# Cross-attention on one core: x and context loaded by columns, scales from column maxima, two buffers of split operands, and the attention loop's first loads moved into the last projection batch

## The chip, the cores and the metric

The kernel runs on one core of a Trainium2 chip. The metric is the device time in microseconds of one execution, the median of several.

## What is computed

The reference (shapes B = 8 batches, S = 512 rows of x, C = 320, T = 508 text tokens and 4 image tokens of E = 512, H = 20 heads of D = 16), cut to what matters:

```
text_ehs, ip_ehs = ctx[:, :-4], ctx[:, -4:]
q, k_t, v_t = heads(x @ W_q), heads(text_ehs @ W_k), heads(text_ehs @ W_v)
probs_t = softmax(q k_t^T * D**-0.5)
text_out = probs_t v_t
k_ip, v_ip = heads(ip_ehs @ W_k_ip), heads(ip_ehs @ W_v_ip)
qsem = l2norm(probs_t @ text_ehs);  sem = qsem @ l2norm(ip_ehs)^T
probs_ip = softmax(q k_ip^T * D**-0.5 + 0.5 * sem) * spatial_mask
out = (text_out + probs_ip v_ip) @ W_out + b_out + x
```

## The kernel before

The work has three phases, one after the other on every engine. Every engine has its program written out by hand and the engines meet at counting semaphores.

*Phase 1*, a loop over the 8 batches. x and the context of a batch are loaded by rows (SP, `x_sb`, `ctx_sb`), transposed on TensorE (fp32 against an identity, `XT_JOB`, `CT_JOB`), and each transposed tile is split on its way out of PSUM into two fp16 parts: ACT writes the high part times a scale (L700, L703), VectorE the remainder (L1017, L1020), into `x_t` and `ctx_t`, of which there is one each. The scale of a batch bounds its largest row norm: VectorE sums squares by row (`squares`, L908) in the v stage of the batch before, TensorE turns the row maxima into a row (`tops`, L1220), VectorE and ACT make scales of it on one partition, and TensorE spreads these over the partitions with a matmul against ones (`scales`, L1232). TensorE's products (L1286) are three fp16 matmuls for each pair of tiles (high by high, high by low, low by high): q (27 matmuls of 512 columns), k (36 of 508), v with the token columns (48 of 324), then the fp32 image token scores (L1344), then the Gram products of the context with itself (48 of 508 to 127 columns) and the transposes of the Gram blocks (L1374). q and k leave as three bf16 parts: ACT the first (L733, L736), VectorE the residual (L1032, `residual`), ACT the middle (L723, `middle`), GpSimd the last (L546); SP stores them, v and the Gram matrix u to DRAM. ACT copies the transposed Gram blocks into `u_sb` (L779).

PSUM's eight banks are given out by hand: a job (j, n) is the n-th use of bank j in a batch, `use` turns it into a count, and TensorE waits in `free` until the bank's use before is drained. The Gram transposes (`GT_JOB`) use bank 3, the first q tile bank 0.

*Phase 2*, the attention, 640 units of 128 rows of one head: scores (L1394), exp on ACT, transposes, then products with v and u. Between the phases SP waits for the stores of parts, v and u, then loads the first two groups of heads, their values and two Gram matrices, with an issue for each copy (`load_group`, L362 and L366); ACT waits for the same three stores. *Phase 3* is the image token softmax and the output projection.

Of the kernel before, what the change touches and what calls it, by code (L numbers as in the profile page):

```python
# [5 lines left out]
def xattn_kernel(  # L6
    nc: bass.Bass,
    x: bass.AP,
    ctx: bass.AP,
# [34 lines left out]
    E = ctx.shape[2]  # L44
    N_IP = 4
    T = ctx.shape[1] - N_IP
# [12 lines left out]
    NC = len(CT)  # L59
    HIP = H * N_IP  # L60
# [28 lines left out]
    with stack:  # L89
# [9 lines left out]
        ones_row = sb("ones_row", [1, P], fp32)  # L99
# [12 lines left out]
        scale = sb("scale", [P, 4], fp32)  # L112
# [3 lines left out]
        x_sb = sb("x_sb", [P, 2, ST, C], fp32)  # L116
# [6 lines left out]
        discard = sb("discard", [P, 2, E], fp32)  # L123
# [12 lines left out]
        q_ring = work[0:KS, 0:2 * GROUP * S // 2].bitcast(bf16).rearrange("p (n h s) -> p n h s", n=2, h=GROUP)  # L136
        k_ring = x_sb[0:KS, :, :, :].rearrange("p r s c -> p (r s c)")[:, 0:2 * GROUP * T // 2].bitcast(bf16)\
# [5 lines left out]
        sumsq = sb("sumsq", [P, TT + ST], fp32)  # L143
        row_max = sb("row_max", [P, 2], fp32)
        w_sums = sb("w_sums", [P, 3], fp32)
        w_scale = sb("w_scale", [P, 3], fp32)
        top = sb("top", [1, 2, 2], fp32)
        w_top = sb("w_top", [1, 3, 3], fp32)
        scale_row = sb("scale_row", [1, 5], fp32)
        w_row = sb("w_row", [1, 3], fp32)  # L150
# [10 lines left out]

        ctx_sb = carve(P, TT * E).rearrange("p (k e) -> p k e", k=TT)
        ctx_t = carve(P, ET * T).bitcast(fp16).rearrange("p (a e t) -> p a e t", a=2, e=ET)
        x_t = carve(P, NC * S).bitcast(fp16).rearrange("p (a c s) -> p a c s", a=2, c=NC)
# [37 lines left out]

        consts_made = sem("consts_made")
# [4 lines left out]
        wq_padded = sem("wq_padded")  # L208
# [3 lines left out]
        w_sums_ready = sem("w_sums_ready")  # L212
        w_top_ready = sem("w_top_ready")
        w_root_ready = sem("w_root_ready")
        w_row_ready = sem("w_row_ready")
        w_hi_split = sem("w_hi_split")
        w_split = sem("w_split")
        top_ready = sem("top_ready")
        top_root_ready = sem("top_root_ready")
        in_hi_split = sem("in_hi_split")  # L220
        ipn_hi_split = sem("ipn_hi_split")
# [13 lines left out]
        sumsq_ready = sem("sumsq_ready")  # L235
        row_max_ready = sem("row_max_ready")
        scale_row_ready = sem("scale_row_ready")
# [49 lines left out]
        FIRST_USES = [0, 0, 0, 0, 0, 0, 0, 4]  # L287
        IP_USES, IP_AFTER = [1, 1, 1, 1, 0, 0, 0, 0], 2
        USES = [3, 3, 3, 3, 3, 3, 3, 4]
# [5 lines left out]
        W_TOP, TOP_0, W_SCALE, SCALE_0 = (7, -3), (7, -2), (7, -1), (7, 0)  # L295
        K_JOB = [(3, 2), (4, 2), (5, 2)]
        V_JOB = [(6, 2), (2, 3), (0, 3), (1, 3)]
        IPS_JOB = (7, 1)
        G_JOB, GT_JOB = [(4, 3), (5, 3), (6, 3), (7, 4)], (3, 3)
# [17 lines left out]
        CTX_COL, X_COL, Q_COL, K_COL = range(4)  # L317
        V_DOWN, SEM_DOWN = 2.0 ** -16, 2.0 ** -13
# [6 lines left out]
        IN_TILES = NC + ET  # L325

        CONSTS = 13 + 1 + D
# [45 lines left out]
        def _(sp):  # L373
            x_in = x.rearrange("b (s p) c -> b p s c", p=P)

            def load_ctx(b):
                for k in range(TT):
                    sp.dma_start(ctx_sb[:, k, :], ctx[b, k * TP:k * TP + P, :]).then_inc(ctx_loaded, 16)

            sp.dma_start(x_sb[:, 0], x_in[0]).then_inc(x_loaded, 16)  # L380
            load_ctx(0)
            for b in range(B):
                sp.dma_start(ip_rows[b * N_IP:(b + 1) * N_IP, 0, :], ctx[b, T:T + N_IP, :]).then_inc(ip_loaded, 16)
# [3 lines left out]
            def store_batch(b):  # L387
# [8 lines left out]

                sp.wait_ge(sem_step, 2 * (b + 1))
# [7 lines left out]
            def next_batch(b):  # L405

                sp.wait_ge(bank_filled[XT_JOB[-1][0]], use(XT_JOB[-1], b))
                sp.dma_start(x_sb[:, 0], x_in[b + 1]).then_inc(x_loaded, 16)
                sp.wait_ge(bank_filled[CT_JOB[-1][0]], use(CT_JOB[-1], b))
                load_ctx(b + 1)  # L410
                store_batch(b)

            sp.wait_ge(row_max_ready, 1)
            next_batch(0)
            with sp.Fori(1, B - 1) as b:
                next_batch(b)


            store_batch(B - 1)
            sp.wait_ge(parts_saved, 1 + 16 * 2 * NC * B)  # L420
            sp.wait_ge(v_saved, 1 + 16 * B)
            sp.wait_ge(u_saved, 1 + 16 * B)
            sp.wait_ge(bank_filled[IPS_JOB[0]], use(IPS_JOB, B - 1))
            for n in range(2):
                load_group(sp, 0, n, n)
                load_values(sp, 0, n, n)
            for par in range(2):
                sp.dma_start(u_sb[:, par, :], u_parts[par]).then_inc(u_loaded, 16)
# [66 lines left out]
        def _(pool):  # L495
# [24 lines left out]
            for d in range(D):  # L520
                if d:
                    pool.wait_ge(consts_made, 14 + d)
# [126 lines left out]
        def _(act):  # L649
# [41 lines left out]
            def batch(b, first, last):  # L691
# [13 lines left out]
                if first:  # L705
                    weight_first(wk, wk_raw, 0)
                    weight_first(wvx, wv_raw, 1)
# [826 lines left out]
```

## Time and profile before

| | us |
|---|---|
| median of 3 runs (lowest, highest) | 1804.03 (1801.88, 1806.68) |
| the profiled execution | 1804.91 |
| its span, first to last instruction | 1803.2 |
| first scores of phase 2 start at | 349.1 |
| TensorE matmul busy, whole span | 1736.2 |
| VectorE, ACT, GpSimd busy, whole span | 1244.6, 1182.8, 1230.7 |

PE is TensorE's matmuls, PEld its weight loads (they overlap), DVE is VectorE, POOL is GpSimd, SP the engine that issues most transfers, an engine's name with a q its sequencer. Busy is the sum of instructions' times. L12 is line 12 of the kernel. PEclk is the granted clock of TensorE as a share of full speed, 1.0 for 2.4 GHz and 0.5 for 1.2 GHz.

### The profile page before, as it was taken

Reading aid. Unit: us, or ns where it says so; the run is one execution under the profiler, and the core shown is the slowest. Engines: PE = TensorE matmul, PEld = TensorE weight load, DVE = VectorE, ACT = ScalarE, POOL = GpSimd, SP = SyncE. Lnnn points to the kernel's source line nnn. Section 1 sums busy time; section 2 is a strip of 40 time slices with the busy share of each in tenths; the row PEclk is TensorE's granted clock in tenths of the full one; section 3 lists DMA queues with packets and bytes.
Section 4 is the critical chain, followed back from the end, with each engine's and each line's share of the span. In section 5 each row is a group of like instructions: output and inputs, shape, how many; then the busy total and the mean of one; then the engine's idle time right before and its main releaser. Section 6 shows DMA issues by size and latency. Waiting matters only on the chain.

```text
span 1803.2 us, 48758 instructions
## 1 busy us (share of the span) xinstructions
PE 1736.2 (96%) x14421; PEld 1103.9 (61%) x14421; DVE 1244.6 (69%) x2872; ACT 1182.8 (66%) x2644; POOL 1230.7 (68%) x1414
## 2 busy tenths in 40 slices
PE   4999999599999999999999999999999999999899
PEld 2767666466666666665666666656566666666455
DVE  5445554277777777777777777767677777777684
ACT  2455455477777777777777777777777777777321
POOL 2122212388888888888788888878888888888310
PEclk7999999799999999999999999999999999999999
DMA  5445554734566445445555555465555445553133
GB/s 161 113 139 142 137 144 123 171 68 92 101 103 119 92 91 111 92 91 92 105 92 100 99 121 92 91 106 92 90 90 113 93 91 103 104 96 66 37 103 101
DMA packets 429986, 187.83 MB, mean 104 GB/s; under 512 B 387128, under 2 KB 417472, under 8 KB 429792
## 3 DMA queue, kind: packets, MB, share of 16 engines
q1 hardware_dynamic: 427488, 183.41, 49.4%
q10 hardware_dynamic: 2304, 2.14, 0.4%
q8 instruction: 84, 1.38, 0.3%
q14 instruction: 110, 0.90, 0.2%
HBM read 67.21 MB, written 34.39 MB: 56 GB/s over the span
## 4 chain that ended last, share of the span: by engine, by line
POOL 37%; PE 35%; issue 22%; DVE 3%; POOLq 1%; ACT 1%; DMA 0%; SPq 0%; ACTq 0%; DVEq 0%
POOL probs L586 16%; POOL probs L593 16%; PE bank L1286 13%; PE bank L1429 6%; PE bank L1430 4%; PE bank L1494 3%; POOL reduced L601 2%; POOL wkv L579 2%; PE bank L1344 2%; PE bank L1394 2%; PE bank L1403 1%; PE bank L1495 1%; POOL reduced L600 1%; PE bank L1434 1%; DVE reduced L1017 1%
## 5 line engine op out<-in xcount | busy, mean ns | idle before, releaser
L1429 PE MATMUL bank<-u_sb,late 127*128 127x508 f16 x2560 | 944.0, 375 | 0.0
L1430 PE MATMUL bank<-u_sb,late 127*128 127x508 f16 (+3 forms) x2560 | 761.1, 297 | 0.0
L1090 DVE TENSOR_REDUCE neg_max<-bank 128x1 f32<-128x508 f32 x640 | 439.3, 687 | 342.0 <-PE bank L1394 341.7
L579 POOL TENSOR_TENSOR wkv<-probs,wkv 128x508 f16<-128x508 f32 x320 | 358.8, 1121 | 199.6 <-ACT wkv L816 199.6
L1428 PE MATMUL bank<-v_ring,late 127*128 127x41 f16 x2560 | 468.1, 183 | 4.4 <-DVE late L1105 4.4
L1099 DVE SCALAR_TENSOR_TENSOR probs<-bank,probs 128x508 f32<-128x508 f32 x640 | 432.9, 677 | 4.6 <-PE bank L1430 4.6
L1428 PEld LDWEIGHTS bank<-v_ring,late 127*128 127x128 f16 x2560 | 246.7, 96 | 233.4 <-DVE late L1105 4.5
L593 POOL TENSOR_TENSOR probs<-probs,late 128x508 f32<-128x508 f32 x320 | 368.6, 1152 | 0.0
L586 POOL TENSOR_TENSOR probs<-probs,wkv 128x508 f32<-128x508 f32 x320 | 357.6, 1118 | 0.0
L1429 PEld LDWEIGHTS bank<-u_sb,late 127*128 127x128 f16 x2560 | 247.8, 97 | 166.2 <-issue 1.1
L1394 PE MATMUL bank<-x_sb,work 96*128 96x508 bf16 x640 | 241.8, 378 | 28.2 <-DMA x_sb<-k_parts 12.2
L1430 PEld LDWEIGHTS bank<-u_sb,late 127*128 127x128 f16 x2560 | 244.8, 96 | 0.0
L807 ACT ACTIVATE probs<-bank,neg_max 128x508 f32<-128x508 f32 x320 | 216.8, 677 | 38.7 <-DVE neg_max L1090 20.8
L796 ACT ACTIVATE exp_bias<-neg_max 128x1 f32<-128x1 f32 x320 | 64.7, 202 | 257.1 <-DVE neg_max L1090 257.1
L1105 DVE SCALAR_TENSOR_TENSOR late<-bank,late 127x512 f16<-127x512 f32 x320 | 219.5, 686 | 7.5 <-ACT late L832 7.5
L816 ACT ACTIVATE wkv<-probs 128x508 f16<-128x508 f32 x320 | 201.4, 629 | 25.1 <-ACT probs L807 17.4
L807 ACT ACTIVATE probs<-bank,exp_bias 128x508 f32<-128x508 f32 x320 | 216.2, 676 | 0.0
L1403 PEld LDWEIGHTS bank<-ident,probs 128*127 128x127 f32 x1280 | 190.9, 189 | 9.2
L823 ACT ACTIVATE late<-probs 128x508 f16<-128x508 f32 x320 | 195.8, 612 | 0.7
L1403 PE MATMUL bank<-ident,probs 128*127 128x128 f32 x1280 | 195.1, 275 | 0.0
L546 POOL TENSOR_TENSOR late<-work,late 128x512 bf16<-128x512 f32 (+3 forms) x48 | 55.2, 1151 | 202.9 <-ACT late L723 202.9
L832 ACT ACTIVATE late<-bank 127x512 f16<-127x512 f32 x320 | 184.9, 578 | 0.0
(166 smaller groups left out, 1803.7 us busy)
## 6 DMA issues: line engine op xcount, KB each, us to landing
x_sb<-k_parts SPq DMA_DIRECT2D x192, 79.4 KB, 3.5
x_sb<-in_x SPq DMA_DIRECT2D x16, 640.0 KB, 5.0
reduced<-in_ctx SPq DMA_DIRECT2D x32, 256.0 KB, 5.1
work<-q_parts SPq DMA_DIRECT2D x32, 240.0 KB, 3.4
u_parts<-u_sb SPq DMA_DIRECT2D x8, 825.5 KB, 4.2
u_sb<-u_parts SPq DMA_DIRECT2D x8, 825.5 KB, 5.4
v_parts<-v_sb SPq DMA_DIRECT2D x8, 820.0 KB, 8.0
v_ring<-v_parts SPq DMA_DIRECT2D x32, 205.0 KB, 3.7
```

What stands on the lines that cost most here:

```text
L579: nc.gpsimd.tensor_tensor(rows[:, 1, :, 0:TP], probs[:, j % PROB_RING, :].rearrange("p (k t) -> p k t", k=TT), rows[:, 0, :, 0:TP], ALU.su ...
L586: nc.gpsimd.tensor_tensor(own, own, flat_rows(at(rnd, j)[1])[:, 1, :, 0:TP], ALU.add).then_inc(odd_weight_ready, 1)
L593: nc.gpsimd.tensor_tensor(own, own, half_hi[:, at(rnd, j)[1] // 2 % RING, :], ALU.subtract).then_inc(even_weight_ready, 1)
L807: nc.scalar.activation(probs[:, j % PROB_RING, :], bank[S_BANK + j % 2][:, 0:T], ACT.Exp, bias=bias[:, j % 4:j % 4 + 1]).then_inc(probs_re ...
L1090: nc.vector.tensor_reduce(neg_max[:, j % 4:j % 4 + 1], bank[S_BANK + j % 2][:, 0:T], AX.X, ALU.max, negate=True)\
L1099: nc.vector.scalar_tensor_tensor(own, bank[Y_BANK + j % 2][:, 0:T], 1.0 if j % 2 == 1 else 2.0 * PROB_SCALE, own, ALU.mult, ALU.mult, accu ...
L1286: last = nc.tensor.matmul(out, stationary(a), moving(m), start=(n == 1), stop=(n == len(SPLIT) * len(terms)))
L1394: nc.tensor.matmul(bank[S_BANK + j % 2][:, 0:T], q_ring[:, n, h, st * P:(st + 1) * P], k_ring[:, n, h, :], start=True, stop=True).then_inc ...
L1403: last = nc.tensor.transpose(bank[PT_BANK + j // 2 % 2][0:TP, k * P:(k + 1) * P], probs[:, j % PROB_RING, k * TP:(k + 1) * TP], ident[:, :])
L1428: nc.tensor.matmul(o, hi_k, v_ring[0:TP, n, h, k, :], start=(k == 0), stop=False)
L1429: nc.tensor.matmul(y, hi_k, u_sb[0:TP, par, GH[k]:GH[k] + T], start=(k == 0), stop=False)
L1430: done = nc.tensor.matmul(y[:, k * TP:T], hi_k, u_sb[0:TP, par, UL[k]:UL[k] + U_COLS[k]], start=False, stop=(k == TT - 1))
```

## The change

- x comes twice: by rows as before for the last addition, and by columns (`x_cols`, three tiles of 128 columns, of which the third holds the last 64 columns twice). The context comes by columns without the image tokens (`ctx_cols`), the image tokens as an input of their own, W_q in three row tiles like x. The layout is made before the launch. The input transposes, their banks and waits go; raw tiles lie in `raw`.
- A batch's scale comes from the absolute maxima of its columns: VectorE reduces both raw tiles after the third residual of the batch before (`column_sums`), squares and adds them by partition, and one matmul against a 128 x 128 of ones (`spread_sums`) adds over partitions, behind the k products. VectorE bounds the sums (`find_top`), ACT takes the root, VectorE makes scales on all partitions.
- `x_t` and `ctx_t` exist twice. The next batch is split in the v stage, two ACT instructions and three of VectorE. The third x tile holds high parts on 64 partitions and remainders on the other 64, so a q tile takes 8 matmuls for 9. The batch loop's body is written out for two batches.
- The jobs are renumbered: Gram transposes go to bank 0, which the next batch's first q tile uses as well.
- SP loads batch b + 2 between the stores of batch b's parts and of its v, and in the last batch the first heads, values and the first Gram matrix of phase 2; the second Gram matrix is loaded in phase 2's first round. ACT enters phase 2 after the stores of the parts alone.
- In the start, the weights' scales go the same way, and VectorE begins without GpSimd's masks.

```diff
-        Q_JOB = [(0, 2), (1, 2), (2, 2)]
-        XT_JOB = [(0, 1), (1, 1), (2, 1)]
-        CT_JOB = [(3, 1), (4, 1), (5, 1), (6, 1)]
-        TOP_JOB, SCALE_JOB = (7, 2), (7, 3)
-        G_JOB, GT_JOB = [(4, 3), (5, 3), (6, 3), (7, 4)], (3, 3)
+        SCALE_JOB = (7, 1)
+        Q_JOB = [(0, 1), (1, 1), (2, 1)]
+        K_JOB = [(3, 1), (4, 1), (5, 1)]
+        V_JOB = [(6, 1), (0, 2), (1, 2), (2, 2)]
+        IPS_JOB = (7, 2)
+        G_JOB, GT_JOB = [(3, 2), (4, 2), (5, 2), (6, 2)], (0, 3)
...
+            def load_columns(b):
+                sp.dma_start(raw_x, x_cols[b]).then_inc(x_loaded, 16)
+                sp.dma_start(raw_ctx, ctx_cols[b]).then_inc(ctx_loaded, 16)
...
+            def columns_of(b):
+                sp.wait_ge(in_lo_split, 2 * b)
...
+                load_columns(b)
+            def first_heads():
+                sp.wait_ge(in_lo_split, 2 * B)
+                sp.wait_ge(parts_saved, 1 + 16 * 2 * NC * (B - 1))
+                sp.wait_ge(v_saved, 1 + 16 * (B - 1))
+                sp.wait_ge(u_saved, 1 + 16 * (B - 1))
+                load_group(sp, 0, 0, 0)
+                load_values(sp, 0, 0, 0)
+                sp.dma_start(u_sb[:, 0, :], u_parts[0]).then_inc(u_loaded, 16)
+                load_group(sp, 0, 1, 1)
+                load_values(sp, 0, 1, 1)
+            columns_of(1)
+            store_batch(0, lambda: columns_of(2))
+            with sp.Fori(1, B - 2) as b:
+                store_batch(b, lambda: columns_of(b + 2))
+            store_batch(B - 2, lambda: None)
+            store_batch(B - 1, first_heads)
...
+            def split_x(b, par):
+                act.wait_ge(scale_ready, b + 1)
+                nc.scalar.activation(x_t[par][:, 0], raw_x, ACT.Identity, scale=scale[:, par, X_COL:X_COL + 1]).then_inc(in_hi_split, 1)
...
             act.wait_ge(parts_saved, 1 + 16 * 2 * NC * B)
-            act.wait_ge(v_saved, 1 + 16 * B)
-            act.wait_ge(u_saved, 1 + 16 * B)
...
+            def column_sums(b):
+                dve.wait_ge(x_loaded, 16 * (b + 1))
+                nc.vector.tensor_reduce(col_max[:, ET:IN_TILES], raw_x, AX.X, ALU.max, apply_absolute_value=True).then_inc(stat_step, 1)
+                dve.wait_ge(ctx_loaded, 16 * (b + 1))
+                nc.vector.tensor_reduce(col_max[:, 0:ET], raw_ctx, AX.X, ALU.max, apply_absolute_value=True).then_inc(stat_step, 1)
+                dve.wait_ge(stat_step, 2 * (b + 1))
+                for col, (c0, c1) in ((CTX_COL, (0, ET)), (X_COL, (ET, IN_TILES))):
+                    nc.vector.scalar_tensor_tensor(col_squares[:, c0:c1], col_max[:, c0:c1], 1.0, col_max[:, c0:c1], ALU.mult,
+                                                   ALU.mult, accum_out=sums[:, col:col + 1]).then_inc(sums_ready, 1)
...
                 for t in range(NC):
                     residual(t)
+                if not last:
+                    column_sums(b + 1)
                 for t in range(NC, 2 * NC):
                     residual(t)
+                if not last:
+                    find_top(SCALE_JOB, b, 0, 2)
...
                     if k == 1 and not last:
-                        squares(b + 1)
+                        make_scales(b + 1, 1 - par)
+                    if k == 2 and not last:
+                        split_x(b + 1, 1 - par)
+                if not last:
+                    split_ctx(b + 1, 1 - par)
...
+                pe.wait_ge(in_lo_split, 2 * b + 1)
                 for m, (c0, cn) in enumerate(CT):
                     j = Q_JOB[m]
-                    pe.wait_ge(bank_drained[XT_JOB[-1][0]], use(XT_JOB[-1], b))
                     free(j)
...
+                free(SCALE_JOB)
...
+                    pe.wait_ge(sums_ready, 2 * (b + 2))
+                    spread_sums(SCALE_JOB, 0, 2)
```

## Rows read from the trace of the kernel before

**Rows 1.** Busy time of each engine and granted clock, by stretch of the span

```profile
core 0: us, PE busy (x) PEld busy (x) DVE busy (x) ACT busy (x) POOL busy (x), PEclk, DMA share, GB/s
31.90:43.90 12.00, 11.96 (x28) 3.27 (x29) 8.06 (x14) 6.27 (x9) 1.15 (x1) 0.51 0.00 0
...
59.20:336.30 277.10, 273.72 (x1668) 190.51 (x1667) 136.11 (x393) 138.61 (x317) 66.26 (x86) 0.98 0.49 133
```

**Rows 2.** The chain that ended last, 150 to 160 us: start, us, what

```profile
151.37 0.31 PE bank L1232 x2
...
154.66 0.50 ACT u_sb L779
...
157.09 0.74 DVE reduced L1017
```

**Rows 3.** Timeline of TensorE: start, us, engine, line, out<-in, [idle before <-releaser]

```profile
121.53 6.54 PE L1286 MATMUL bank<-reduced,wq 128*128 128x512 f16 x27 [0.31 <-DVE reduced L1017]
...
146.42 2.79 PE L1286 MATMUL bank<-reduced 128*127 128x508 f16 x12
...
154.29 1.50 PE L1295 MATMUL bank<-ident,x_sb 128*128 128x128 f32 x12
...
157.88 6.54 PE L1286 MATMUL bank<-reduced,wq 128*128 128x512 f16 x27 [0.34 <-DVE reduced L1017]
164.35 8.01 PE L1286 MATMUL bank<-reduced,wkv 128*128 128x508 f16 x36
172.29 6.83 PE L1286 MATMUL bank<-wkv,reduced 128*127 128x324 f16 x48
```

**Rows 4.** Timeline of all engines, the last batch's Gram stage

```profile
329.78 6.74 PE L1286 MATMUL bank<-reduced 128*127 128x508 f16 x48
...
336.96 0.93 ACT L779 ACTIVATE u_sb<-bank 127x127 f16<-127x127 f16 x3
```

**Rows 5.** Groups of instructions: busy us, mean ns of one

```profile
L1090 DVE TENSOR_REDUCE neg_max<-bank 128x1 f32<-128x508 f32 x640 | 439.3, 687 | 342.0 <-PE bank L1394 341.7
...
L968 DVE SCALAR_TENSOR_TENSOR wkv<-probs,w_scale,wkv 128x1280 f16<-128x1280 f32 x1 | 1.5, 1535 | 0.0
...
L677 ACT ACTIVATE wkv<-probs,w_scale 128x1280 f16<-128x1280 f32 x1 | 1.4, 1371 | 0.0
...
L968 DVE SCALAR_TENSOR_TENSOR wq<-probs,w_scale,wq 128x960 f16<-128x960 f32 x1 | 1.2, 1219 | 0.3 <-ACT wq L677 0.3
L677 ACT ACTIVATE wq<-probs,w_scale 128x960 f16<-128x960 f32 x1 | 1.1, 1094 | 0.7 <-DVE w_scale L962 0.7
```

**Rows 6.** Timeline of all engines, the third residual of a batch

```profile
165.75 0.74 DVE L1032 SCALAR_TENSOR_TENSOR work<-bank,scale,late 64x512 f32<-64x512 f32 x1 [1.41 <-ACT late L733]
```

**Rows 7.** Who waited for whom, whole span: us in total, times, longest us

```profile
ACT v_sb L749 <- PE bank L1286: 37.1, 32, 8.7
...
DVE top L916 <- PE bank L1220: 28.4, 8, 5.2
ACT ip_scores L757 <- PE bank L1344: 26.9, 8, 3.6
...
PE bank L1394 <- issue: 8.6, 3, 3.3
```

**Rows 8.** Timeline of all engines, the start of the kernel

```profile
2.57 0.78 ACTq L653 DMA_DIRECT2D reduced<-in_L_xattn_W_v  x1
...
51.83 0.43 PE L1253 MATMUL bank<-ident,reduced 32*128 32x32 f32 x4
...
59.18 9.19 PE L1286 MATMUL bank<-wkv,reduced 128*127 128x324 f16 x48
```

**Rows 9.** DMA issues: KB each, median us to landing

```profile
reduced<-in_L_xattn_W_v ACTq DMA_DIRECT2D x1, 640.0 KB, 12.3
```

**Rows 10.** The chain that ended last, 300 to 360 us

```profile
337.91 3.54 DMA u_parts<-u_sb
...
349.10 0.60 PE bank L1394
```

**Rows 11.** Timeline of TensorE, the Gram stage of the sixth batch

```profile
255.65 4.22 PE L1286 MATMUL bank<-reduced 128*127 128x508 f16 x12
```

More of the change, by code:

```diff
@@ L98, in xattn_kernel @@
         ident16 = sb("ident16", [P, P], fp16)
[L99 removed]
+        ones = sb("ones", [P, P], fp32)
         headmask = sb("headmask", [P, NC, H], fp32)
@@ L111, in xattn_kernel @@
         vw = sb("vw", [96, B, C], fp32)
-        scale = sb("scale", [P, 4], fp32)
+        scale = sb("scale", [P, 2, 4], fp32)
         kept_scale = sb("kept_scale", [P, B, 2], fp32)
@@ L403, in store_batch @@
                 sp.dma_start(u_parts[b], u_sb[:, 1, :]).then_inc(u_saved, 16)
[L405 to L428, printed above, removed]
+            def columns_of(b):
+                sp.wait_ge(in_lo_split, 2 * b)
+                apart(sp)
+                load_columns(b)
[15 more added lines that the diff above has]
+            store_batch(B - 1, first_heads)
             sp.wait_ge(flat_padded, 1)
@@ L670, in _ @@
+            act.wait_ge(w_scale_ready, 1)
+            weight_first(wq, wq_raw, WQ_COL)
+            split_x(0, 0)
+            act.wait_ge(bank_drained[W_JOB[0]], use(W_JOB, 0))
+            nc.scalar.activation(bound[:, 3:5], top[:, 3:5], ACT.Sqrt, scale=IN_TOP ** -2).then_inc(w_root_ready, 1)
+            split_ctx(0, 0)
+            act.wait_ge(w_scale_ready, 5)
+            weight_first(wk, wk_raw, WK_COL)
             act.wait_ge(ip_step, 1)
             nc.scalar.activation(ip_stat[:, 1:2], ip_stat[:, 0:1], ACT.Sqrt).then_inc(ip_root, 1)
-            act.wait_ge(wq_padded, 1)
@@ L688, in ip_tokens, with batch @@
                 act.wait_ge(bank_drained[1], ip_use(1))
-            def batch(b, first, last):
-                act.wait_ge(bank_drained[SCALE_JOB[0]], use(SCALE_0, 0) if first else use(SCALE_JOB, b - 1))
-                apart(act)
-                for t in range(IN_TILES):
-                    j = (XT_JOB + CT_JOB)[t]
-                    act.wait_ge(bank_filled[j[0]], use(j, b))
-                    if t < NC:
-                        cn = CT[t][1]
-                        nc.scalar.activation(x_t[0:cn, 0, t, :], bank[j[0]][0:cn, 0:S], ACT.Identity,
-                                             scale=scale[0:cn, X_COL:X_COL + 1]).then_inc(in_hi_split, 1)
-                    else:
-                        nc.scalar.activation(ctx_t[:, 0, t - NC, :], bank[j[0]][:, 0:T], ACT.Identity,
-                                             scale=scale[:, CTX_COL:CTX_COL + 1]).then_inc(in_hi_split, 1)
-                if first:
-                    weight_first(wk, wk_raw, 0)
-                    weight_first(wvx, wv_raw, 1)
+            def batch(b, par, first, last):
                 def ip_columns():
@@ L772, in batch @@
                                              scale=2.0 * GRAM_SCALE).then_inc(gram_hi2_split, 1)
-                    if k == 0 and not last:
-                        scale_root(b + 1)
                 act.wait_ge(bank_filled[GT_JOB[0]], use(GT_JOB, b))
@@ L1306, in batch, with products @@
-                if first:
-                    first_scales()
+                def products(out, terms, more=()):
+                    pairs = [(stationary(a), moving(m)) for stationary, moving in terms for a, m in SPLIT] + list(more)
+                    for n, (stationary, moving) in enumerate(pairs):
+                        last = nc.tensor.matmul(out, stationary, moving, start=(n == 0), stop=(n == len(pairs) - 1))
+                    return last
+                x_b, ctx_b = x_t[par], ctx_t[par]
@@ L1376, in batch @@
                 last.then_inc(bank_filled[GT_JOB[0]], 1)
-            batch(0, True, False)
-            with pe.Fori(1, B - 1) as b:
-                batch(b, False, False)
-            batch(B - 1, False, True)
+            batch(0, 0, True, False)
+            with pe.Fori(0, B // 2 - 1) as pair:
+                for par in (1, 0):
+                    batch(2 * pair + 2 - par, par, False, False)
+            batch(B - 1, 1, False, True)
             for j in range(8):
```

407 lines of the change are left out of this document (178 added, 229 removed).

## The prediction

> **What bounds the kernel now.** I read the busy share by stretch first, then the chain that ended last where one batch of the first phase gives way to the next. From 59.2 to 336.3 us TensorE is busy 273.72 of 277.1 us at a granted clock of 0.98 [rows 1]: the batch loop is TensorE's. The second phase and the projections are not edited, so the question is what leaves TensorE's own stream in the first 349 us, and what it waits for then.
>
> The chain at a boundary [rows 2] runs ACT's copies of the transposed Gram blocks (L779, to 154.66 + 0.50 = 155.16), ACT's first split, VectorE's remainders (L1017, to 157.09 + 0.74 = 157.83), TensorE. TensorE's timeline of the batch [rows 3] fills that in: the input transposes start at 154.29, the q products at 157.88, the k products at 164.35, the v products at 172.29. One undisturbed batch takes 157.88 - 121.53 = 36.35 us.
>
> **The change, part by part.**
>
> *The batch boundary.* Transposes, their PSUM banks and the splits that follow them leave the boundary; the split operands wait in the other buffer. But the q products of the next batch now use bank 0 right after the Gram transposes, which have moved from bank 3 to bank 0. So TensorE no longer waits for VectorE, but for ACT's L779 copies. Where that ends when no scale work sits between the Gram products is shown by the last batch, which has none already: Gram products start at 329.78, L779 ends at 336.96 + 0.93 = 337.89 [rows 4], 8.11 us; with 0.06 us of release the next q products can start 8.17 us after the Gram start. Before it was 157.88 - 146.42 = 11.46 us [rows 3]. Gain 3.29 us for each of 7 boundaries, 23.0 us. About 1 us of idle TensorE stays in each.
>
> *q products.* 9 matmuls per output tile become 8 (the third row tile carries x's high part and its remainder on 128 partitions). 27 of them take 164.35 - 157.88 = 6.47 us [rows 3], 0.240 us each; the share of pure streaming is less, so I take 0.22 us for each of the 3 removed: 0.65 us in each of 7 batches, 4.6 us.
>
> *Scales.* Two matmuls with the ones move behind the k products, where nothing else hides them: 0.31 us as the chain gives for the old pair, L1232 [rows 2]. It was inside the 11.46 us and is gone from the 8.17, so it counts again: 6 x 0.31 = 1.9 us lost (batch 0's belongs to the start).
>
> *VectorE in the k stage.* The column maxima need reductions of 3 x 512 and 4 x 508 elements. The nearest row is the 128x508 reduction at 687 ns [rows 5]; its elements at the rate by which two VectorE rows differ ((1535 - 1219) / 320 = 0.98 ns an element) leave some 0.19 us fixed, so 1.7 + 2.2 us, with two short operations 4.4 us. They stand between the third and the fourth residual. The third ends 165.75 + 0.74 = 166.49 [rows 6], 2.1 us after the k products begin; so the sums are ready 6.5 us after it, and TensorE, which wants them after 7.94 us, has 1.4 us of slack. Queued behind them are residuals 4 to 6, ACT's middle parts of these and GpSimd's L546; residual 6 waits for the last k product anyway. Bounds for the reductions: 2.0 us (twice as fast as the row) costs nothing less, as they are off TensorE's path; at twice the price (7.9 us) TensorE stands 2.6 us a batch.
>
> *The splits in the v stage.* ACT gets 1536 and 2032 elements; by L677 (1094 ns for 960, 1371 for 1280 [rows 5]) 1.6 + 2.0 us. VectorE gets 1.3 + 0.7 + 2.3 us by L968, and loses the seven remainders of L1017 and L1020 and the squares of L908. Cover: ACT now waits 37.1 us in 32 waits for v products and 26.9 in 8 for the token scores, 8.0 us a batch; VectorE 28.4 in 8 for the old maxima [rows 7]. In us after the k start: the four v tiles are filled 1.7 apart (6.83 / 4 [rows 3]) from 9.9 on; the scales stand behind VectorE's work on the second, about 13.7; ACT's x split to 15.3, two v tiles 16.5, context split 18.5; VectorE's x remainders to 18.4, the fourth tile 19.1, context remainders 21.3. The token scores are full when the Gram products start, 146.42 - 121.53 - 6.47 + 0.3 = 18.7 [rows 3], and VectorE is wanted one Gram tile and two copies later, about 22.5. So ACT has 0.2 us of slack there and more behind, since its next tile is 2.6 us off, VectorE 1.2. If that cover goes, each us over reaches TensorE through L779.
>
> *Loads.* Two issues in place of five, some 1.78 MB, behind the parts' stores and ahead of the v store on SP's queue. They leave at about 21.3 us after the k start and are read some 14 us later; a wait there would hold SP's v and u stores too, and ACT awaits those only a batch later. I price it at nothing.
>
> *Start of the kernel.* VectorE no longer waits for GpSimd's masks. The last thing late is w_v: issued at 2.57 us, 12.3 us to landing [rows 8, 9], 14.9; with 0.2 MB more ahead, 15.3. Squares 1.5 us (16.8), four short scale operations (17.2), ACT's w_q split 1.1 and x split 1.6 (19.9), VectorE's x remainders 2.0: q products at 22.0 instead of 31.9. Their 27 filled a stretch of 12.0 us at clock 0.51 [rows 1]; 24 take 10.7 us, to 32.7. If the clock again rises some 11.7 us into the stretch, the k products, 7.94 us (172.29 - 164.35), lose 0.5 us: 41.1. Scale matmuls 41.4; token work 51.83 to 59.18 [rows 8], 7.35 us: 48.8. Gain 59.18 - 48.8 = 10.4 us.
>
> *Into the second phase.* L779 ends at 337.89; then come the u store's 3.54 us, its issues and loads, and the first scores at 349.10 [rows 10]. Now SP issues the first two groups, values and u in the last v stage (some 10 us of issues from 324 on), done before the Gram products end; ACT waits for the parts' stores alone. The first scores follow the last drains: 338.0. Gain 11.1 us. The v store starts some 5 us later, and nobody waits for it but SP's later load. What is late next is the pipeline fill up to the first unit, 12.3 us on ACT and GpSimd, which stays.
>
> **Sum.** 10.4 + 23.0 + 4.6 - 1.9 + 11.1 = 47.2 us. Profiled execution: 1804.91 - 47.2 = 1757.7. It lies 0.9 us over the median of 1804.03; from there 1756.8. I take 1757.
>
> **The clock.** The trace has cold spells beside the start: at 255.65 twelve Gram products took 4.22 us against 2.79 [rows 11, 3], 1.4 us lost; batch 1 had one too, and batch 0 lost 9.19 - 6.83 = 2.4 us in its v stage [rows 8, 3]. The sum keeps three such spells. The Trainium skill (TensorE: Matmul & The Clock Gate, HAM oscillation — how this bites in real kernels) describes a kernel whose clock falls again at every tile because TensorE waits for data in each one; a wait in each batch is what this change leaves. Its section Part 4: PE-mode transpose says that transposes don't count as busy for the clock as other matmuls do, which speaks the other way, since transposes are what goes. By the first the sum would be 40, by the second alone 47 or a little more; no row here separates them.
>
> **Rivals.**
> 1. *The clock falls in every batch* (0.17). For: the new 1 us idle follows the Gram transposes, close on low-activity work. Against: TensorE idles 0.34 us there already [rows 3], and the spells begin elsewhere, at the token scores. Five more, 5 x 1.43 = 7.2 us: 1764.
> 2. *VectorE becomes the bound of the k stage* (0.10): reductions slower than the row, at double price 7 x 2.6 = 18 us back: 1775. Against: two VectorE forms agree on the rate.
> 3. *The doubled loop body costs instruction supply, or the first phase's early loads collide* (0.08). TensorE stood 8.6 us in 3 waits for nothing but issue in the second phase [rows 7]; three such in the new pair loop give 8.6 us: 1766. Against: the old batch loop shows none.
> 4. *Slower than before* (0.03): the same place as rival 2, the column sums late, whether by the reductions or because the loads land late. The price per batch must exceed the slack by 47.2 / 7 = 6.7 us, that is column sums ending 8.1 us later than reckoned, 12.5 us for 4.4. At 14 us: 7 x (14 - 4.4 - 1.4) = 57 back, 1814. The loads of before (x and context together) landed within some 8 us of their first issue, far inside 14.
>
> My forecast has 0.62. **Range.** Likeliest case alone: 1753 to 1761 (start within 2 us either way, spells from one to five). With rivals 1 and 3 inside, and no spells and a warm second phase below, 1749 to 1768. What a measurement of this kernel can tell from no change is about 0.3%, 5.4 us: faster 0.96, same 0.02, slower 0.02 (rival 4 split).
>
> **What the profile after would show.** Right: no fp32 transposes at a boundary; q products about 1 us after the Gram transposes, released by L779's counterpart; undisturbed batches of 36.35 - 3.29 - 0.65 + 0.31 = 32.7 us; first q products near 22 us; first scores near 338 - 36.2 = 302 us, within 0.3 us of the last Gram copy; a phase from first scores to end as long as before, 1803.2 - 349.1 = 1454.1 us. Wrong: TensorE waiting after the k products for the sums, or at the q products for remainders; ACT's token score copy late; more spells at clock 0.5; a second phase longer than 1454.1 us, which I have argued only from its code being the same.

## The result, and the profile after

The changed kernel takes 1834.34 us (median of 4 runs, 1817.98 to 1848.06), the kernel before 1804.12 us beside it (4 runs, 1801.88 to 1806.68). The ratio is 1.014 with a 95% interval of 1.010 to 1.0185: slower by 1 to 2%, where I had forecast 1757 us. The profiled execution is the longest of the four, 1848.06 us with a span of 1846.3; it counts as a slow one and is left out of the ratio, so of the loss that its trace shows below, some 14 us are more than the median run has.

The page of the changed kernel: busy time, the two queues that bring instructions (packets, MB, share), and the chain that ended last.

```profile
span 1846.3 us, 47756 instructions
PE 1737.4 (94%) x14154; PEld 1095.5 (59%) x14154; DVE 1235.3 (67%) x2726; ACT 1178.7 (64%) x2604; POOL 1245.5 (67%) x1413
...
q8 instruction: 102, 1.67, 0.4%
...
q14 instruction: 181, 1.47, 0.3%
...
POOL 39%; PE 30%; issue 26%; DVE 2%; POOLq 1%; ACT 1%; DMA 1%; ACTq 0%; DVEq 0%
```

The kernel before has 84 and 110 packets on these two queues, which its page gives in the same place:

```profile
q8 instruction: 84, 1.38, 0.3%
...
q14 instruction: 110, 0.90, 0.2%
```

TensorE's timeline after, for the start, one batch and its boundary, and the change of phase (it answers to [rows 3, 4, 8, 10]):

```profile
23.12 7.88 PE L1245 MATMUL bank<-reduced,wq 128*128 128x512 f16 x24 [4.50 <-DVE reduced L930]
...
41.16 9.13 PE L1230 MATMUL bank<-reduced 128*128 128x32 f32 x48 [1.28 <-issue]
...
105.29 5.90 PE L1245 MATMUL bank<-reduced,wq 128*128 128x512 f16 x24 [1.02 <-ACT u_sb L780]
111.12 8.01 PE L1245 MATMUL bank<-reduced,wkv 128*128 128x508 f16 x36
119.06 0.38 PE L1207 MATMUL bank<-sums,ones 128*128 128x2 f32 x2
119.31 6.81 PE L1245 MATMUL bank<-wkv,reduced 128*127 128x324 f16 x48
125.95 3.87 PE L1302 MATMUL bank<-reduced,work 128*128 128x80 f32 x24
129.75 8.43 PE L1245 MATMUL bank<-reduced 128*127 128x508 f16 x48
138.01 0.52 PE L1320 MATMUL bank<-ident,u_sb 127*127 127x127 f16 x6
139.55 0.82 PE L1245 MATMUL bank<-reduced,wq 128*128 128x512 f16 x3 [1.02 <-ACT u_sb L780]
...
302.55 9.06 PE L1245 MATMUL bank<-reduced 128*127 128x508 f16 x48
311.47 0.54 PE L1320 MATMUL bank<-ident,u_sb 127*127 127x127 f16 x6
313.03 0.60 PE L1341 MATMUL bank<-raw 96*128 96x508 bf16 x2 [1.02 <-ACT u_sb L780]
```

The first phase did about what the change is made of. A batch takes 139.55 - 105.29 = 34.26 us (before 36.35), the transposes are gone from the boundary, and the first scores come at 313.03 us, 36.1 us earlier than the 349.10 of [rows 10]. All of that and more is lost again later. Busy time from the first scores to the last ones and from there to the end, before and then after (columns as in [rows 1]):

```profile
349.10:1664.80 1315.70, 1299.66 (x12003) 821.04 (x12004) 985.65 (x2216) 993.68 (x2229) 1116.20 (x1267) 0.99 0.53 98
1664.80:1803.20 138.40, 127.99 (x595) 72.69 (x591) 93.72 (x194) 30.84 (x64) 30.19 (x23) 1.00 0.26 80
```

```profile
313.00:1704.80 1391.80, 1325.50 (x12003) 832.09 (x12004) 987.91 (x2216) 994.90 (x2229) 1116.36 (x1267) 0.98 0.52 93
1704.80:1846.30 141.50, 131.09 (x595) 73.79 (x592) 93.73 (x194) 30.84 (x64) 30.18 (x23) 0.98 0.26 78
```

The same 12003 matmuls take 76.1 us longer, and TensorE is busy only 25.8 us more in them (some of it at the lower clock): it stands idle 66.3 us, not 16.0. The busy times of VectorE, ACT and GpSimd have not changed. So no work was added; something waits. Who waited for whom in the whole span after (us in total, times, longest):

```profile
ACT probs L807 <- issue: 76.8, 15, 7.3
PE bank L1341 <- ACT probs L807: 47.9, 19, 4.9
...
PE bank L1341 <- issue: 14.2, 5, 3.1
...
DVE neg_max L1079 <- issue: 10.7, 17, 2.3
```

ACT is held up 15 times by nothing but its own instruction supply ("issue": it waits for nothing that the profile shows), 5.1 us each time, and its second-phase loop jumps back once a round. In [rows 7] TensorE had 8.6 us of that kind in 3 waits; ACT and VectorE had none in the second phase. ACT's timeline around one jump back, before and then after:

```profile
1006.28 0.22 ACT L838 ACTIVATE out_raw<-bank 128x82 f32<-128x82 f32 x1
1008.59 0.69 ACT L807 ACTIVATE probs<-bank,neg_max 128x508 f32<-128x508 f32 x1 [2.09 <-DVE neg_max L1090]
```

```profile
828.36 0.22 ACT L838 ACTIVATE out_raw<-bank 128x82 f32<-128x82 f32 x1
834.10 0.68 ACT L807 ACTIVATE probs<-bank,neg_max 128x508 f32<-128x508 f32 x1 [5.52 <-issue]
```

The two loops hold the same instructions. What differs is where they stand: in ACT's program as it is compiled the loop takes instructions 415 to 763 before and 448 to 796 after, since the unrolled and doubled batches ahead of it are longer.

### The profile page after: what moved, and what is told of

It is laid out like the page before. It is cut to its first block, busy times and chain, and to the rows that moved or that the text cites. A ratio compares the mean times of both kernels' runs of the same rounds, so it can differ in the third digit from the quotient of the medians.

```text
span 1846.3 us, 47756 instructions
## 1 busy us (share of the span) xinstructions
PE 1737.4 (94%) x14154; PEld 1095.5 (59%) x14154; DVE 1235.3 (67%) x2726; ACT 1178.7 (64%) x2604; POOL 1245.5 (67%) x1413
## 4 chain that ended last, share of the span: by engine, by line
POOL 39%; PE 30%; issue 26%; DVE 2%; POOLq 1%; ACT 1%; DMA 1%; ACTq 0%; DVEq 0%
POOL probs L587 17%; POOL probs L594 17%; PE bank L1245 13%; PE bank L1376 4%; PE bank L1441 3%; PE bank L1377 3%; POOL reduced L602 2%; POOL wkv L580 2%; PE bank L1302 2%; PE bank L1442 1%; POOL reduced L601 1%; PE bank L1341 1%; PE bank L1350 1%; DMA reduced<-in_L_xattn_W_v 1%; PE bank L1230 0%
## 5 line engine op out<-in xcount | busy, mean ns | idle before, releaser
L1376 PE MATMUL bank<-u_sb,late 127*128 127x508 f16 x2560 | 957.0, 380 | 0.0
L1377 PE MATMUL bank<-u_sb,late 127*128 127x508 f16 (+3 forms) x2560 | 771.0, 301 | 0.0
L1375 PEld LDWEIGHTS bank<-v_ring,late 127*128 127x128 f16 x2560 | 249.4, 97 | 247.1 <-issue 21.5
L1341 PE MATMUL bank<-raw 96*128 96x508 bf16 x640 | 244.7, 383 | 63.1 <-ACT probs L807 47.9
L807 ACT ACTIVATE probs<-bank,neg_max 128x508 f32<-128x508 f32 x320 | 216.9, 678 | 92.9 <-issue 76.8
L1350 PEld LDWEIGHTS bank<-ident,probs 128*127 128x127 f32 x1280 | 195.9, 193 | 9.6
L1381 PEld LDWEIGHTS bank<-v_ring,late 127*128 127x128 f16 x2560 | 131.6, 97 | 78.1 <-issue 4.7
```

The lines of the kernel that those rows point to most:

```text
L807: nc.scalar.activation(probs[:, j % PROB_RING, :], bank[S_BANK + j % 2][:, 0:T], ACT.Exp, bias=bias[:, j % 4:j % 4 + 1]).then_inc(probs_re ...
L1341: nc.tensor.matmul(bank[S_BANK + j % 2][:, 0:T], q_ring[:, n, h, st * P:(st + 1) * P], k_ring[:, n, h, :], start=True, stop=True).then_inc ...
L1350: last = nc.tensor.transpose(bank[PT_BANK + j // 2 % 2][0:TP, k * P:(k + 1) * P], probs[:, j % PROB_RING, k * TP:(k + 1) * TP], ident[:, :])
L1375: nc.tensor.matmul(o, hi_k, v_ring[0:TP, n, h, k, :], start=(k == 0), stop=False)
L1376: nc.tensor.matmul(y, hi_k, u_sb[0:TP, par, GH[k]:GH[k] + T], start=(k == 0), stop=False)
L1377: done = nc.tensor.matmul(y[:, k * TP:T], hi_k, u_sb[0:TP, par, UL[k]:UL[k] + U_COLS[k]], start=False, stop=(k == TT - 1))
```

## The experiments

Two theories to begin with. **A, the place of the loop:** what a jump back costs depends on where the loop's instructions lie, so moving it by 33 alone does the damage. **B, the changed data path:** new buffer addresses, the early loads and the changed semaphores slow the second phase, and the "issue" label misleads. The tool for it is an increment of a semaphore that nobody watches, which is one instruction on ACT and takes 0.07 us there; put where ACT waits anyway, in the last batch, it moves what follows and nothing else.

**e1: the kernel before, moved by 33**

```
+for _ in range(n if last else 0):              # n = 7, 7, 7, 6 and 6 in five places: 33 in all
+    apart(act)                                 # act.sem_inc(unwatched, 1)
 act.wait_ge(bank_filled[j[0]], use(j, b))      # here ACT's v loop, last batch
```

> The kernel before, with 33 semaphore increments that nobody waits for added to ACT's program in the last batch of phase 1, where ACT waits for TensorE anyway; they put ACT's loop of phase 2 at exactly the place in ACT's program that it has in the changed kernel (instructions 448 to 796 for 415 to 763). Nothing else of the change is in it. Theory A (the place of the loop in the program makes each jump back wait for instructions): ACT idle before L807's counterpart for nothing but issue, 15 times some 5 us, and with it 40 to 80 us more than before, some 1845 to 1880. Theory B (the stall comes from something the change does in phase 2 or to the transfers): no such idle time, 1804 within 3 us.

Measured: 1849.17 us against 1803.14, ratio 1.025 (1.022 to 1.028). ACT waits for issue 61.1 us in 15 waits:

```profile
ACT probs L814 <- issue: 61.1, 15, 4.7
...
PE bank L1401 <- issue: 11.5, 4, 3.0
```

A is shown: 33 idle instructions make the old kernel 46 us slower, with no part of the change in it. VectorE has no such wait here, so in the changed kernel its waits are a second item.

**e2: the changed kernel, moved by 88 more** (loop at 536 to 884)

> The changed kernel with 88 such increments on ACT in the last batch's v and Gram stage (18 at most in one place, some 1 us each), which put the loop at 536 to 884. Theory A, if what matters is that the loop then touches fewer blocks of instructions: the 15 waits go and phase 2 takes the 1454 us of before; the end at 313 + 1454 + 2 = some 1769. Theory B: as the changed kernel, 1818 to 1848, with ACT's 77 us of idle time.

Measured: 1782.12 us, ratio 0.987 (0.982 to 0.9915). ACT's waits fall to 18.5 us in 7, and first to last scores take 1340.6 us, not 1391.8. The direction is right, and the time is 13 us over the 1769 expected.

**e3: the changed kernel with the Gram transposes in bank 7**, which is free there, so that the next q products need not wait for ACT's last copies

```
-USES = [3, 2, 2, 2, 2, 2, 2, 2]
+USES = [2, 2, 2, 2, 2, 2, 2, 3]
-G_JOB, GT_JOB = [(3, 2), (4, 2), (5, 2), (6, 2)], (0, 3)
+G_JOB, GT_JOB = [(3, 2), (4, 2), (5, 2), (6, 2)], (7, 3)
```

> The changed kernel with the Gram transposes in bank 7 in place of bank 0, so that the next batch's first q tile doesn't wait for ACT's copies; ACT's program loses two instructions, so its loop stays where it stalls. The wait of 1.02 us at each of 7 boundaries goes: 7 us. If that wait is also what brings the cold spell of every batch (8.43 us of Gram products where 6.74 are undisturbed), 7 x 1.7 = 12 us more; phase 1 then ends at 313 - 19 = 294, else at 306. If the spells come from the low-activity stages and where they fall in time, they move or vary in number instead. The whole: some 1810 to 1830, as phase 2 keeps its stalls.

**e4: both, bank 7 and 88 increments**

> Both edits of the two runs before: bank 7 for the Gram transposes, and 88 increments on ACT. By theory A the sum of both: 1769 less 7 (wait alone) to 19 (wait and spells), 1750 to 1762. By theory B 1810 to 1840.

Measured: e3 1797.0 us, ratio 0.997 (0.994 to 0.999), 13 us below the range expected; e4 1771.78 us, ratio 0.983 (0.980 to 0.985), 10 us above it. TensorE's timeline of e3:

```profile
94.31 6.74 PE L1245 MATMUL bank<-reduced 128*127 128x508 f16 x48
100.89 0.52 PE L1320 MATMUL bank<-ident,u_sb 127*127 127x127 f16 x6
101.24 5.89 PE L1245 MATMUL bank<-reduced,wq 128*128 128x512 f16 x24
...
125.69 6.74 PE L1245 MATMUL bank<-reduced 128*127 128x508 f16 x48
```

Without the wait of 1.02 us the batch takes 31.4 us, and the 48 Gram products keep to 6.74 us in five of eight batches; in the changed kernel they took 8.1 to 9.1 us in seven of eight. The first scores come at 297.1 us. So bank 7 saves 2.9 us in such a batch: 1.2 us at the boundary and 1.7 us in a Gram stage that keeps its clock. How the wait and the slow Gram stage hang together is not shown. The granted clock falls to 0.5 only some 24 us behind the wait, as the token scores end (129.8 us in the changed kernel), and the other kernels agree in number alone: with the wait the Gram products are slow in seven (the changed kernel, e2) and five (e10) batches of eight, without it in one to three (e3, e4, e7, e8, e9, e12). The first three batches of e10 have the wait of 1.02 us and keep to 6.74 us.

e3 had a surprise: its ACT loop lies two instructions earlier than the changed kernel's, because its program is two instructions shorter, and ACT's waits under this label went from 76.8 us to 21.3 in 8 (and 5.2 in 2 one instruction on), while first to last scores still took 1356.3 us. That asks for the sequencer's own records. Time from the end of ACT's jump to the start of each of the loop's first five instructions, one typical jump of each kernel:

```
kernel     loop begins at   1st  2nd  3rd  4th  5th, us after the jump
before          415         2.4  2.5  2.6  2.6  3.2
after           448         2.5  2.6  6.0  6.0  6.6
e1              448         2.4  2.5  4.6  4.6  5.2
e3              446         2.4  2.5  2.6  2.6  6.1
e4              534         2.8  2.9  2.9  3.0  3.5
```

Each of the five kernels waits 2.4 us or more behind a jump, the one of before too, where it lies beside a wait that is there anyway. In the changed kernel and e1 two instructions follow and then there is a second wait; in e3 four follow. 448 + 2 = 446 + 4 = 450: a block of instructions ends there, and the next one is fetched only after the first has come. VectorE shows the other half. Its loop jumps without any wait before (first instruction 0.2 us after the jump, all 14 times looked at), but after 2.7 to 3.0 us in the changed kernel, where it lies 16 instructions earlier by the trace. The packets on q14 are 0.90 MB / 110 = 8.2 KB. If a block is 128 instructions, VectorE's loop of 324 can lie in three blocks before and in four after.

**Theory C:** instructions of ACT and VectorE come in blocks of 128, with borders at 450, 578, 706 of ACT's program. A loop that touches three blocks stays in the buffer and jumps free. One that touches four waits 2.4 us for the first block, and if it begins just ahead of a border, again for the second.

**e5 and e6: the kernel before with 161 and with 165 increments on ACT**, four instructions apart

> The kernel before with 161 idle semaphore increments in ACT's last batch of the first phase, nothing else: its second-phase loop then begins at instruction 576 of ACT's program, 128 past the place of the run with 33. Theory C (instructions arrive in blocks of 128, with borders at 450, 578, 706, ...; a jump back to a block that is gone waits about 2.4 us for it, and if the loop's first instruction lies two before a border, a second time for the next block): two instructions after each jump, then a second wait of 2 us or more, ACT idle for issue alone some 4 to 5 us in each of 15 rounds, 1849 us. If blocks were 256 long with the border at 450 (the next at 706), no second wait and 1803 us. If what counts is only how far ACT's program is stretched, slower than 1849.

> The same with 165 increments, four more: the loop begins at instruction 580, two past a border, and its 349 instructions touch three blocks of 128 instead of four. Theory C, with the further claim that three blocks stay in the engine's buffer: no wait at all after ACT's jump (the first instruction behind it after 0.3 us, not 2.4), fewer instruction packets (some 4 a round fewer), and a time as before, 1798 to 1804, since TensorE is busy 82.0 of 82.0 us in a round before. Rival (a far jump always costs the 2.4 us, and only the border behind it matters): 2.4 us stay and 1803. Any theory in which the place does not matter so finely: the same as the run with 161.

Measured: e5 1851.93 us, ratio 1.0275 (1.0235 to 1.032); e6 1801.99 us, ratio 0.998 (0.996 to 1.000), both against 1803.33. ACT's timeline at a jump of e5, then of e6:

```profile
1025.70 0.22 ACT L845 ACTIVATE out_raw<-bank 128x82 f32<-128x82 f32 x1
1029.99 0.68 ACT L814 ACTIVATE probs<-bank,neg_max 128x508 f32<-128x508 f32 x1 [4.07 <-issue]
```

```profile
1009.79 0.22 ACT L845 ACTIVATE out_raw<-bank 128x82 f32<-128x82 f32 x1
1009.91 0.68 ACT L814 ACTIVATE probs<-bank,neg_max 128x508 f32<-128x508 f32 x1
```

At 576, two ahead of a border, the second wait is back (2.4, 2.5, 4.6); at 580 there is no wait at all (0.2, 0.3, 0.4). Four idle instructions are worth 50 us. The queue says the same: 112 packets in e5, and in e6

```profile
q14 instruction: 42, 0.34, 0.1%
```

that is 68 fewer than before in 15 rounds. And with ACT's jumps free the old kernel is no faster, as expected: TensorE bounds its rounds.

**e7: e4 with 16 idle increments on VectorE**, which restore its place

```
 if last:
+    for _ in range(16):
+        apart(dve)
     dve.wait_ge(bank_filled[SCALE_JOB[0]], use(SCALE_JOB, b))
```

> The changed kernel with the Gram transposes in bank 7 and 88 increments on ACT (1771.8 us before this), and 16 idle increments in VectorE's last batch, which bring VectorE's second-phase loop to its place in the kernel before. Theory C: VectorE's jump back waits 0.2 us again, not 2.8, its 15 us of idle time for issue in 18 waits go, and some 4.7 instruction packets a round with them. ACT still waits 2.5 to 3 us at its own jump. Scores to scores falls from 1335.8 towards the 1315.7 of before; 1752 us, at least 1760 if VectorE's waits were hidden behind ACT's. If VectorE's waits come from the queue being busy and not from its place: no change, 1772.

**e8: the same with 137 increments on ACT in place of 88** (loop at 583)

> The changed kernel with the Gram transposes in bank 7, 137 increments on ACT (loop at 583 to 931, three blocks) and 16 on VectorE. Theory C: neither engine waits at its jump, the phase from first to last scores is that of the kernel before, 1315 us or a few less, and with the first scores at 291 the time is 291 + 1454 = 1745 us, up to 1750. Rival (the second phase is longer for another reason too, as TensorE's own place or the changed loads): 1760 or more.

Measured: e7 1761.33 us, ratio 0.977 (0.9735 to 0.980); e8 1760.95 us, ratio 0.976 (0.974 to 0.979). VectorE's waits for issue are gone, q14 is back at 110 packets (180 in e4), and e7 is 10.5 us faster than e4. That is 9 us over the first number expected, 1752, though first to last scores fell as expected, from 1335.8 us to 1320.9: the first scores came at 298.45 us, in e4 at 290.43, as e7's profile has three slow Gram stages and e4's one. e8 gains nothing over e7, although it has 41 packets where e7 has 110: with VectorE free, ACT's 2.5 us are hidden as they were before. e8 misses its 1745 by 16 us. TensorE's waits in its second phase:

```profile
PE bank L1350 <- issue: 13.9, 5, 3.2
PE bank L1350 <- ACT probs L814: 6.3, 5, 2.6
```

TensorE stands five times for its own instructions (8.6 us in 3 before), and the rounds in which it does so take 86 to 88 us, the others 81.6; the lower clock that follows such a stop is in that.

**e9 and e10: TensorE's loops moved too**, by 218 increments ahead of its program; e9 is e8 with them, e10 the changed kernel as it is (bank 0) with 135, 16 and 218

> The run with bank 7 and both loops placed (1760.95 us), and 218 idle increments ahead of everything on TensorE, which has nothing to do in the first 15 us. In that run TensorE still stood for issue alone 13.9 us in 5 waits (before 8.6 in 3), and the rounds of these waits took 86 to 88 us, the others 81.6. Theory C taken over to TensorE, with 256 instructions to a block and seven blocks that stay (a matmul counted as two instructions, its weight load and itself; a round is then 1654 long and fits where it begins at most 138 past a border): before, the two loops of the pair began 136 and 1 past a border and fit, in the changed kernel 46 and 167, so the second one does not. With 218 more they begin 8 and 129 past one. Expected: no wait at the second loop's jump back, the two or three waits of 2.5 us at the outer jump stay, 1748 us. Rival (TensorE's waits hang on something else than its place): the same five waits and 1761 us.

> The changed kernel as it is, Gram transposes in bank 0, with all three loops placed by idle increments alone (135 on ACT, 16 on VectorE, 218 on TensorE). It asks what the change is worth when the second phase runs as before. The first scores come at 313 us as in the changed kernel, and 1454 us on top give 1767 us if TensorE's theory holds, 1778 if only ACT's and VectorE's does. Had anything of the changed data path (loads of the first heads, the buffers' new addresses) made the second phase slower, 1785 or more.

Measured: e9 1777.87 us (ratio 0.988, 0.985 to 0.992), e10 1789.14 us (0.993, 0.9905 to 0.995). Both miss what was expected of them, and e10 as it stands would speak for theory B. But a price was wrong in both. An increment on TensorE takes 0.15 us, not the 0.07 of ACT, and the start waits for them:

```profile
34.51 0.56 PE L1219 MATMUL bank<-sums,ones 128*128 128x3 f32 x2 [34.51 <-issue]
38.14 0.59 PE L1219 MATMUL bank<-sums,ones 128*128 128x2 f32 x2 [3.07 <-DVE late L948]
43.23 7.66 PE L1257 MATMUL bank<-reduced,wq 128*128 128x512 f16 x24 [4.50 <-DVE reduced L937]
```

The first q products start at 43.23 us where the changed kernel has 23.12, so 20.1 us of each are the experiment's own. Behind that, e9's first to last scores take 1310.8 us (e8 1325.7), with two long waits of TensorE at the outer jump and none at the loops' own. In e10 it is 1318.8 us with four, two of them at the loops' own jumps. Taking off the 20.1 us, e10 stands at 1769.0: an estimate of what the changed kernel takes with a second phase like before's. That phase is 3.1 us longer than before's 1315.7, with one more long wait of TensorE in it, so little is left for the data path (theory B).

**e11 and e12: is it TensorE's place?** e11 is the kernel before with 16 increments ahead of TensorE's program, e12 is e8 with 108 small matmuls there in place of increments

```
+pe.wait_ge(ones_made, 1)
+for _ in range(108):
+    nc.tensor.matmul(bank[6][0:32, 0:2], ones[:, 0:16].bitcast(bf16), ones[:, 16:17].bitcast(bf16), start=True, stop=True)
```

> The kernel before with 16 idle increments ahead of everything on TensorE (2.4 us, at 0.15 us each, where it has nothing to do), nothing on the other engines. The two runs before left it open whether TensorE's waits follow its place: one had none at the loops' own jumps, the other two in six. Theory C for TensorE: the pair's loops now begin 152 and 17 past a border of 256; the first one no longer fits (138 is the last that does), so its jump back waits 2.5 to 3.2 us in each of the three turns of the outer loop instead of once, with a round of 85 to 88 us each time for one of 82: 8 to 12 us more than before, 1812 us, and some 8 more instruction packets on TensorE's queue. Rival (TensorE's waits come from chance in the fetch, not from the place): 1803 us, three waits as before.

> The run with bank 7 and ACT's and VectorE's loops placed (1760.95 us), with TensorE's place moved by 217 instructions at a lower price than increments: 108 matmuls of two columns, 32 by 128, ahead of everything, at something under 0.1 us each, done by the time the first sums are ready, 15 us in. Nothing reads what they write. Theory C for TensorE: the phase from first to last scores is 15 us shorter, as in the run with 218 increments beside the one without, and nothing is lost at the start, where TensorE may even be warmer: 1748 us. If TensorE's waits come by chance: 1761 us.

Measured: e11 1804.74 us, ratio 1.001 (0.998 to 1.003), three waits as before: theory C for TensorE, with the border that I had worked out, is refuted there. e12 1756.29 us (1750.53 to 1757.8), ratio 0.974 (0.971 to 0.978), the fastest of all, though 8 us over the 1748 expected. The 108 matmuls took 3.04 us, TensorE's issue waits are three, and first to last scores take 1316.6 us against 1325.7. The start gave part of it back: the first scores come at 299.48 us, in e8 at 296.58. TensorE's timeline of e12 at the start:

```profile
1.08 3.04 PE L1217 MATMUL bank<-ones 128*32 128x2 bf16 x108 [1.08 <-POOL ones L499]
```

Who waited for whom in e12, TensorE for its own supply:

```profile
PE bank L1355 <- issue: 10.3, 3, 3.5
```

All six kernels with the changed kernel's own TensorE program (after, e2, e3, e4, e7, e8) have five of these waits, the three with it moved by 218 or 217 have two (e9), four (e10) and three (e12), the four with the old one three or four, and e11 three. So the number of waits goes with TensorE's place, but not with it alone: e9 and e10 stand at the same place and have two and four. That the place is the cause is not shown for TensorE, nor by what rule it would be.

## Why the prediction was wrong

**The step that failed** is the last sentence of the prediction: a second phase of 1454.1 us, "which I have argued only from its code being the same". It took 1391.8 + 141.5 = 1533.3 us. The code is the same and its place is not. 79.2 us of loss against 36.1 us of gain make the +43.1 us of the profiled execution (1804.91 to 1848.06). e1 shows that the place of ACT's loop alone costs 46 us in the kernel before. VectorE's place adds 10.5 us (e7 against e4), and TensorE's waits go with 9 to 15 us of the second phase (1325.7 us in e8, 1316.6 in e12, 1310.8 in e9), by a cause that stays open. From first to last scores alone, the profiles give 49.7 us for ACT (1365.4 in e1), 14.9 for VectorE and these 9 to 15, together 74 to 80 of the 76.1 lost. Each is one execution, and the profiled one of the changed kernel lies 14 us above its median, so that the three come out so close is in part luck. One thing may add to ACT's part: q14 serves ACT and VectorE (181 packets after, 110 with VectorE at its old place in e7, 41 with ACT's loop moved as well in e8), and ACT's second wait is a little longer where VectorE fetches too (a median of 2.9 us over the 14 jumps after, 2.4 in e1).

**Rival 3** had the right resource. It looked for it in the first phase's doubled loop, at 8.6 us, and I argued against it from the old batch loop showing none. The doubled loop did cost nothing: ACT goes on 0.1 us behind its jumps. The batch loop was not the one to look at: any loop behind code whose length changes is moved. The profile of before held the warning. ACT's jump already cost 2.4 us there, under a wait labelled VectorE.

The Trainium skill (Runtime: NRT & Kernel Launch, Instruction fetch mechanics) says that a taken branch whose target is outside the two pages in the buffer waits for a fetch. The traces agree that a jump can wait for a fetch. It gives pages of 256 instructions; here e5 and e6 show a border 128 after the one at 450, and ACT's loop of 349 instructions stays when it touches three blocks of 128. The measurement decides.

**The batch boundary** came as worked out: the q products start after 1.02 us of idle time, released by L780, and 9.80 us after the Gram products' start, close to 8.17 and the 1.69 us that these took longer than 6.74. **q products:** 24 in 5.90 us for 27 in 6.54. **VectorE in the k stage** and **the splits:** the reductions took 1735 and 2253 ns (1.7 and 2.2 forecast), ACT's splits 1573 and 2002 (1.6 and 2.0), and TensorE waits for neither. **Scales** took 0.25 us of TensorE's stream for 0.31. **Into the second phase:** the first scores follow the last copy by 0.05 us; 11.1 us gained, as forecast. The loads cost nothing: behind the start no engine waits for one. In the last batch one wait stands in no term of the sum, 0.68 us before the token scores, released by VectorE.

**The start** gained 9.0 us, not 10.4. The first q products came at 23.12 (22.0 forecast), as w_v was read at 16.43, not 15.3. Of the clock I had the place wrong: it rose within the q products (7.88 us for 10.7), and fell again as the token matmuls began, which took 9.13 us.

**The clock.** The sum kept three spells, and rival 1, at 0.17, is what happened: from the second batch on every Gram stage took 8.12 to 9.06 us, where 6.74 is undisturbed. The batch takes 34.26 us, not 32.7. I had argued that a wait of 0.34 us did no harm before. With 1.02 us the spells came, and e3, which removes only this wait, has them in three batches of eight; but as said at e3, three batches of e10 have the wait and no spell, so with the wait the spells are more frequent, and more is not shown. The start (1.4 us) and the spells beyond the three that the sum kept (some 10 us) are about the 11.1 us between 36.1 and 47.2. The Trainium skill's oscillation (TensorE: Matmul & The Clock Gate, HAM oscillation — how this bites in real kernels), named in the prediction, has a fall of the clock in every tile, as the changed kernel has one in seven of eight batches; but there it follows directly on the wait, and here it comes 24 us later.

With the second phase held to its old speed, then, the change is worth some 33 us (e10, 1769.0 against the 1801.95 beside it) where 47 were forecast, and with bank 7 for the Gram transposes 46 us (e12, 1756.29 against 1802.62). That the second comes close to the 47 forecast is no merit of the forecast: e12 has another bank, 153 idle increments and 108 idle matmuls in it.

## What to carry to other kernels

When code ahead of a loop changes in length, the loop is part of the change: compare each engine's "issue" waits and the instruction packets of before and after, and look at the two or three instructions behind each jump back. A loop that just fits is worth keeping where it fits, if need be with idle instructions placed where the engine waits anyway; price them per engine. A bank that is shared across a stage boundary cost nearly three microseconds a batch here for one of waiting, so use a free one.

## What the runs showed of the hardware

- ACT holds a loop that touches three blocks of 128 instructions, and not one that touches four. Its loop of 349 jumps in 0.2 us at 580 and 583, in 2.4 to 3.3 us at 415, 534 and 536, and with a second wait of 2 to 5 us at 446, 448 and 576. VectorE's loop of 324 jumps in 0.2 us at its old place and in 2.7 to 3.1 us 16 instructions earlier (after, e4); its borders were not measured.
- A jump's fetch can be invisible: 2.4 us in each round of the kernel before, and removing it (e6) changed the time by 1.3 us, inside the noise.
- An idle semaphore increment takes 0.07 us on ACT and 0.15 us on TensorE; a bf16 matmul of two columns, issued back to back, 0.028 us (3.04 us for 108).
- TensorE has 2 to 5 waits of some 2.5 to 3.5 us for its instructions in the second phase, each with a round 3 to 6 us longer, and their number differs between places of its program and at one place too. With blocks of 256 and a matmul counted as two instructions I could explain the five of the changed kernel, but not e11 nor the two at the loops' own jumps in e10.
